# A routed macaron block: second choices by half groups directly behind the first, and both reciprocal roots of the attention stage on VectorE

## What is computed

```python
x = x + 0.5 * ffn(layernorm(x))
x = x + attn(layernorm(x))
x = x + 0.5 * ffn(layernorm(x))

def layernorm(x):  m, v = mean(x), var(x);  return (x - m) / sqrt(v + 1e-5)

def attn(x):       # linear attention, 16 heads of 8 features
    q, k, v = elu(x @ Wq + bq) + 1, elu(x @ Wk + bk) + 1, x @ Wv + bv
    return (q @ (k^T v per head)) @ Wp + bp

def ffn(x):        # 16 experts, the two largest scores of a token, and a shared expert
    scores = softmax(x @ gate_w + gate_b);  top_vals, top_idx = top_k(scores, 2)
    y = sum over the two choices of top_val * ((silu(x @ w1[e] + b1[e]) * (x @ w3[e] + b3[e])) @ w2[e] + b2[e])
    return y + (silu(x @ sw1 + sb1) * (x @ sw3 + sb3)) @ sw2 + sb2
```

## Time and profile before

| what | value |
|---|---|
| time, median of 3 runs | 983.95 us (983.07 to 985.2) |
| profiled execution | 988.44 us |
| its span, first to last instruction | 986.7 us |
| mean granted clock of TensorE | 0.914 |
| busy: TensorE / VectorE / ScalarE / GpSimd | 792.0 / 579.8 / 470.2 / 562.8 us |
| scatters of tokens (L346) | 256, 992 ns each |
| roots on GpSimd (L353, L375) | 16, 28.7 us in all |

### The profile page before, as it was taken

One profiled execution on the slowest core, in us unless ns is written; L12 is line 12 of the kernel. 1 busy time (PEld: TensorE's weight loads), 2 busy tenths in 40 slices (PEclk: granted clock), 3 DMA queues, 4 the chain that ended last, 5 costly groups with the idle time before them and its releaser, 6 DMA issues. The chain is left out here.

```text
span 986.7 us, 20333 instructions
## 1 busy us (share of the span) xinstructions
PE 792.0 (80%) x5348; PEld 705.0 (71%) x5349; DVE 579.8 (59%) x2112; ACT 470.2 (48%) x967; POOL 562.8 (57%) x584
## 2 busy tenths in 40 slices
PE   2899899847999999806788999899934999999920
PEld 2677777737999999804567777787824999999910
DVE  7688876624555555545557776666722555555536
ACT  3356556313555555415456657665302555555500
POOL 1347777762777777722044266575772777776730
PEclk9799999977999999958779999999976999999965
DMA  9912221132333333241021111010132333333349
GB/s 274 141 45 72 65 68 54 52 92 72 100 105 100 105 101 96 83 164 63 1 65 60 49 44 39 31 48 31 50 97 60 96 101 100 103 102 99 96 166 374
DMA packets 83816, 90.45 MB, mean 92 GB/s; under 512 B 20391, under 2 KB 69421, under 8 KB 82733
## 3 DMA queue, kind: packets, MB, share of 16 engines
q1 hardware_dynamic: 64046, 45.41, 18.3%
q0 software_dynamic: 17408, 35.95, 10.8%
q10 hardware_dynamic: 2304, 8.39, 2.1%
HBM read 47.45 MB, written 44.37 MB: 93 GB/s over the span
## 5 line engine op out<-in xcount | busy, mean ns | idle before, releaser
L1246 POOL DMA_INDIRECT ys<-e_y,e_x x288 | 276.5, 960 | 132.0 <-issue 89.0
L346 POOL DMA_INDIRECT xs<-f_xrow,f_slot x256 | 254.0, 992 | 131.9 <-issue 72.8
L1365 PE MATMUL e_py<-w,e_at 97*128 (+1 forms) x1152 | 152.1, 274 | 0.0
L1365 PEld LDWEIGHTS e_py<-w,e_at 97*128 97x128 f32 (+1 forms) x1152 | 139.9, 191 | 0.1
L1270 DVE TENSOR_TENSOR e_a<-e_pu,e_sil 128x352 f32<-128x352 f32 x144 | 75.6, 525 | 98.2 <-ACT e_sil L1296 96.9
L1277 DVE TENSOR_SCALAR e_y<-e_py,e_x 128x128 f32<-128x128 f32 x288 | 87.8, 347 | 58.9 <-PE e_py L1365 57.9
L1290 ACT ACTIVATE e_xth<-e_px 128x256 fp32r<-128x256 f32 x144 | 55.4, 385 | 131.3 <-PE e_px L1329 130.6
L1296 ACT ACTIVATE e_sil<-e_pu 128x352 f32<-128x352 f32 x144 | 66.9, 464 | 91.0 <-PE e_pu L1342 91.0
L1028 PEld LDWEIGHTS f_pz<-sw,f_gated 128*128 128x128 f32 (+1 forms) x768 | 99.4, 191 | 11.4 <-issue 3.2
L1340 PE MATMUL e_pu<-w13h,e_xth 128*128 x288 | 107.2, 372 | 0.0
L843 ACT ACTIVATE f_sil<-f_phg,sb 128x512 f32<-128x512 f32 (+1 forms) x96 | 65.0, 684 | 84.4 <-PE f_phg L1014 83.7
(11 more groups left out here) (166 smaller groups left out, 1362.7 us busy)
## 6 DMA issues: line engine op xcount, KB each, us to landing
e_x<-xs SPq DMA_DIRECT2D x288, 65.0 KB
f_yt<-ys SPq DMA_DIRECT2D x16, 512.0 KB, 4.6
c_yt<-ys SPq DMA_DIRECT2D x8, 1024.0 KB, 10.4
ys<-e_y,e_x POOLq DMA_INDIRECT x288
xa<-in_attn_x ACTq DMA_DIRECT2D x8, 512.0 KB, 10.2
xs<-f_xrow,f_slot POOLq DMA_INDIRECT x256, 2.3
out<-xa ACTq DMA_DIRECT2D x8, 512.0 KB
f_raw<-in_ffn_w SPq DMA_DIRECT2D x32, 88.0 KB
```

What stands on the lines that cost most here:

```text
L346: pool.indirect_dma_start(xs, bass.IndirectOffsetOnAxis(slot[:, q, i:i + 1], 0), xrow[:, i, :], None).then_inc(done, 16)
L1246: pool.indirect_dma_start(ys, bass.IndirectOffsetOnAxis(xin[r][:, t, D:D + 1].bitcast(I32), 0), y[r][:, t, :], None).then_inc(sent[r], 16)
L1365: last = pe.matmul(p_y[r][:, t * D:(t + 1) * D], at[r][0:rows_, q], w2, start=c == 0, stop=c == 1, skip_group_check=True)
```

## The change

First, second choices follow the first choices of their own group, by half groups: GpSimd sends the 8 first choices of group `g`, then the 4 second choices of each half as soon as that half is rewritten. `rewrite` takes a half group `c`; four semaphores count the landed first choices by half groups. In VectorE's order the rewrite of group `s-1` now stands in step `s` of front 0, and in front 1 the first half of group `s` at the end of step `s`, the second half of group `s-1` in step `s` behind `phi_q`. Second, both roots of front 1 are taken on VectorE, each directly behind its variance, with its shift directly behind it; the Newton chain becomes a function `root` for both.

```diff
+        sent0 = [sem(f"f{n}_sent0{r}") for r in range(4)]
 @block.gpsimd
-                def send(g, q, done):
-                    for i in range(g * GT, (g + 1) * GT):
+                def send(c, q, done):
+                    for i in range(c * CHUNK, (c + 1) * CHUNK):
...
-                    send(g, 0, sent0[g % 3])
+                    for c in (2 * g, 2 * g + 1):
+                        send(c, 0, sent0[c % 4])
...
-                    pool.wait_ge(rewrote, g + 1)
-                    pool.sem_inc(passed, 1)
-                    send(g, 1, sent1)
...
-                if n == 0:
-                    for g in range(GROUPS + 1):
-                        first(g)
-                        second_choice(g - 1)
-                else:
-                    for s in range(-3, GROUPS + 2):
-                        first(s - 1)
-                        if 0 <= s + 1 < GROUPS:
-                            scales(s + 1)
-                        if s + 3 < GROUPS:
-                            scales_a(s + 3)
-                        second_choice(s - 2)
+                    for c in (2 * g, 2 * g + 1):
+                        pool.wait_ge(rewrote, c + 1)
+                        pool.sem_inc(passed, 1)
+                        send(c, 1, sent1)
+
+                for g in range(GROUPS):
+                    first(g)
+                    second_choice(g)
 @block.vector
+                def root(y, x, done):
+                    dve.tensor_scalar(half[:], x[:], -0.5, None, ALU.mult)
+                    dve.tensor_scalar(y[:].bitcast(I32), x[:].bitcast(I32), -0.5, MAGIC_ROOT,
+                                      ALU.mult, ALU.add).then_inc(newton, 1)
+                    at = 9 * roots[0]
+                    roots[0] += 1
+                    for i in range(3):
+                        dve.wait_ge(newton, at + 3 * i + 1)
+                        dve.tensor_tensor(sq[:], y[:], y[:], ALU.mult).then_inc(newton, 1)
+                        dve.wait_ge(newton, at + 3 * i + 2)
+                        dve.tensor_tensor(sq[:], sq[:], half[:], ALU.mult).then_inc(newton, 1)
+                        dve.wait_ge(newton, at + 3 * i + 3)
+                        last = dve.scalar_tensor_tensor(y[:], sq[:], 1.5, y[:], ALU.add, ALU.mult)
...
+                def scales_a(g):
+                    wait(dve, xhr_a, 2 * (g - 1))
+                    dve.wait_ge(var_a, g + 1)
+                    root(rs_a[g % 2], ve_a, rstd_a)
...
-                def rewrite(g):
-                    dve.wait_ge(sent0[g % 3], 16 * GT * (g // 3 + 1))
-                    dve.wait_ge(exp2, g + 1)
+                def rewrite(c):
+                    if not 0 <= c < CHUNKS:
+                        return
+                    part = slice(c * CHUNK, (c + 1) * CHUNK)
+                    dve.wait_ge(sent0[c % 4], 16 * CHUNK * (c // 4 + 1))
+                    dve.wait_ge(exp2, c // 2 + 1)
...
 step(s), front 0
                     gates(m)
                     if s == GROUPS:
                         tables()
+                    rewrite(2 * (s - 1))
                     gates(m + 1)
...
                     gates(m + 2)
-                    if s >= 2:
-                        rewrite(s - 2)
+                    rewrite(2 * (s - 1) + 1)
                     if gating:
                         hot(s)
 step_1(s), front 1
-                    if 0 <= s + 2 < GROUPS:
-                        shifts_a(s + 2)
                     if attending:
                         phi_q(a, 0)
                         phi_q(a, 1)
+                    rewrite(2 * (s - 1) + 1)
+                    if attending:
                         phi_k(a, 0)
                         phi_k(a, 1)
                     if gating:
                         largest(s)
...
                         variances(f)
+                        scales(f)
+                        shifts(f)
                     outs(2 * (s - 1) - 1)
                     if gating:
                         sums(s)
                         places(s)
                     gates(m + 2)
-                    if 0 <= s - 2 < GROUPS:
-                        rewrite(s - 2)
                     if b < GROUPS:
                         residual(b)
                     gates(m + 3)
-                    if attending:
-                        shifts(f)
...
                     if b < GROUPS:
                         variances_a(b)
+                        scales_a(b)
+                        shifts_a(b)
                     if gating:
                         low(2 * s)
                     gates(m + 5)
+                    rewrite(2 * s)
                     if gating:
                         low(2 * s + 1)
```

More of the change, by code:

```diff
@@ L116, in build @@
         k.region = sb("region", [P, E])
-        k.nhalf = sb("nhalf", [P, GT])
         k.expert_of = sb("expert_of", [1, SLOT_TILES])
@@ L224, in front @@
             sem(f"f{n}_{m}") for m in names)
-        sent0 = [sem(f"f{n}_sent0{r}") for r in range(3)]
+        sent0 = [sem(f"f{n}_sent0{r}") for r in range(4)]
         def of(g):
@@ L308, in _ @@
                     pool.memset(k.onesb[:], 1.0)
-                    pool.memset(k.nhalf[:], -0.5)
                     pool.memset(k.ones_e[:], 1.0).then_inc(tail, 1)
@@ L348, in send @@
                             None).then_inc(done, 16)
-                def scales(g):
-                    pool.wait_ge(var, g + 1)
-                    wait(pool, xhr, 2 * (g - 2))
-                    pool.tensor_tensor(rs[g % 3][:], ve[g % 2][:], k.nhalf[:], ALU.pow
-                                       ).then_inc(rstd, 1)
                 def first(g):
@@ L421, in variances @@
                                       ).then_inc(var, 1)
-                def scales(g):
-                    y, x = rs[g % 3], ve[g % 2]
-                    wait(dve, xhr, 2 * (g - 2))
-                    dve.wait_ge(var, g + 1)
+                roots = [0]
+                def root(y, x, done):
                     dve.tensor_scalar(half[:], x[:], -0.5, None, ALU.mult)
@@ L439, in scales @@
                             last.then_inc(newton, 1)
-                    last.then_inc(rstd, 1)
+                    last.then_inc(done, 1)
+                def scales(g):
+                    wait(dve, xhr, 2 * (g - 2))
+                    dve.wait_ge(var, g + 1)
+                    root(rs[g % 3], ve[g % 2], rstd)
+                def scales_a(g):
+                    wait(dve, xhr_a, 2 * (g - 1))
+                    dve.wait_ge(var_a, g + 1)
+                    root(rs_a[g % 2], ve_a, rstd_a)
                 def shifts(g):
@@ L512, in places @@
                     dve.tensor_copy(slot[:, :, of(g)], at[:]).then_inc(slots, 1)
-                def rewrite(g):
-                    dve.wait_ge(sent0[g % 3], 16 * GT * (g // 3 + 1))
-                    dve.wait_ge(exp2, g + 1)
-                    if g == 0:
+                def rewrite(c):
[4 more added lines that the diff above has]
+                    dve.wait_ge(exp2, c // 2 + 1)
+                    if c == 0:
                         dve.wait_ge(dests, 1)
-                    dve.scalar_tensor_tensor(xrow[:, of(g), D + 1:D + 2], rec[:, of(g)].unsqueeze(2),
-                                             0.5, wtop[:, of(g)].unsqueeze(2), ALU.mult, ALU.mult)
-                    dve.tensor_copy(xrow[:, of(g), D:D + 1].bitcast(I32),
-                                    dest1[:, of(g)].unsqueeze(2)).then_inc(rewrote, 1)
+                    dve.scalar_tensor_tensor(xrow[:, part, D + 1:D + 2], rec[:, part].unsqueeze(2),
+                                             0.5, wtop[:, part].unsqueeze(2), ALU.mult, ALU.mult)
+                    dve.tensor_copy(xrow[:, part, D:D + 1].bitcast(I32),
+                                    dest1[:, part].unsqueeze(2)).then_inc(rewrote, 1)
                 def low(c):
```

8 lines of the change are left out of this document (removed).

## The result

The changed kernel takes **997.5 us** (median of four runs, 996.7 to 1000.25) against 984.58 before (a median of four; the 983.95 above was that of the first three): a ratio of 1.013, 95% interval 1.0108 to 1.0152. It is slower by some 13 us, outside the predicted range (976 to 993) and on the side that had a chance of 0.31. Its profiled execution took 997.78 us with a span of 996.1, 9.4 us longer than the profiled execution before.

What follows compares the result with a forecast made beforehand. GpSimd's scatter queue was taken to end both fronts, with TensorE, ScalarE and VectorE handing work on inside. Front 0 −8.6, front 1 +2.9 and clock +3.6 gave −2.1 us from 983.95: 981.9 us, range 976 to 993.

Steps and rivals of the forecast that it cites:

- gains nothing here: Front 1, steps 1 to 4: removing TensorE's stall for normalised rows saves nothing, since TensorE then waits for VectorE instead.
- Rival 3: VectorE hides everything: no waits but in steps 6 and 7, both ends gain nearly in full, 965.2 us; chance 0.10.
- the waits of 2 to 5 us in steps 6 to 8 of front 1: Sign expected in the changed profile: VectorE waiting this long at the rewrite for the scatters' DMA.
- 2.3 us to landing by the median: Landing time taken for a half group's last scatter, part of the 12.4 us from slots to second half's rewrite.
- Rival 1: Scatters land late before the second half's rewrite: 13.5 us from slots to rewrite, 993.1 us in all; chance 0.24.
- The term of +1.0: Front 0's price for late rewrites: 0.5 us in step 1 and 0.5 us over steps 2 to 5 together.
- My test for rival 1: Front 0: TensorE's waits for the weight split stay near 1.2 us a step; growth to 2 means rival 1 holds.
- it has 3.11 us to spare: Front 1, steps 1 to 4: VectorE's room for 4.6 us of added work; 1.5 too many, 6.1 us over four steps.
- the +1.8 us for the last stretch: Front 1, step 7 to 8: the rewrite delays the gate product by 4.4 us, of which 2.6 come back.
- step 6 to 7 (+4.9): Front 1: no attention work stands ahead, so VectorE waits in the rewrite before `largest(7)`, 4.9 us later.
- TensorE's clock: Front 1: longer waits lower the granted clock, +2.6 us in step 7 and +1 elsewhere; 3.6, bounds 0 and 7.6.
- The fourth rival: GpSimd and VectorE share an SBUF read port: +2 us for each of eleven roots in front 1, 1004 us; chance 0.03.

Runs made afterwards that it cites:

- scatters_alone: Changed kernel's shorter scatter queue, but front 1's roots stay on GpSimd, its order written out, and rewrites are placed to avoid waits for landings: 962.1 us, ratio 0.9757.
- norm_stats_later: scatters_alone with the norm's root on VectorE behind the first down-product sum, and the next attention group's statistics moved behind the second sum: 956.2 us, ratio 0.9708.
- norm_root: scatters_alone with only the root of the norm ahead of the gate on VectorE, its shift behind it, placed as in the change: 973.4 us, ratio 0.9889.
- all_later: Changed kernel with all rewrites placed later in both fronts, both roots left on VectorE: 979.9 us, ratio 0.9934.
- one_newton: all_later with one Newton step in place of three in each root of front 1: 959.4 us, ratio 0.9736.

## Why the prediction was wrong

**Right.** GpSimd's queue ended both fronts, the half groups took it off the end, and the padding copies are the cap: −9.6 and −13.6 us, confirmed by scatters_alone (−2.4%, 23.8 us). Right was also that VectorE pays, in waits for landings and in room for the roots. That the earlier shift "gains nothing here" held in the changed kernel, but not once the room was there: the way of norm_stats_later is 6.2 us shorter than that of scatters_alone. Rival 3 (VectorE hides everything) was rightly held small. Of the signs named, the waits of 2 to 5 us in steps 6 to 8 of front 1 came as 0.4 to 3.4 us.

**Front 0: the way from slots to rewrite.** The first step that failed is "2.3 us to landing by the median", and with it the 12.4 us. The way was 13.9, since the wait is for the eighth landing and no other, and the eighth met a 1.4 us packet of TensorE's own program in six groups. A median over all scatters cannot show that one place is always late; yet the trace of the kernel before had it: the packet stands there at 67, 89 and 111 us, beside eighth first choices that started at 66.11, 89.02 and 110.53, and where the seven ahead of the last took 2.3 to 2.7 us to land, the view of its line says

```profile
DMA to landing us min/median/max: 3.5/3.5/3.5
```

Rival 1 (landings late, 13.5 us, 993.1) had place and sign, and nearly the price, but the price by luck: its row, set aside because of the copies in flight, has no instruction packet beside it (724 to 729). The term of +1.0 measured 7.4. Of the 7.1 us by which the copies start later, 3.4 are one step in which TensorE waited 2.39 us for the split weights and fell to half clock; the prediction had put the clock into front 1 alone. My test for rival 1, waits for the split near 2 us, was met in three steps (1.82, 2.34 and 2.39).

**Front 1, steps 1 to 4: the room.** The second step that failed is "it has 3.11 us to spare" (busy 14.54 of 17.65 us): it counts the gaps up to the key product. TensorE meets VectorE earlier, at the two sums of the down products: at the first in most steps of the changed kernel (the root starts at 590.10, the sum at 592.26, TensorE waits 2.36 us), at the second when the root stands behind the first. Up to the second the gaps are 1.23 us; what is left behind that sum cannot be used by work that must stand ahead of it. So the norm's root alone was too much, as norm_root shows. Steps 1 to 4 were priced at 6.1 us; from key product to key product they took 5.6, 2.3, 2.6 and 2.0 us longer, 12.5 together, and in all_later, where no rewrite in them waits, still 12.1. Part of this is half clock (below).

**Front 1, the end.** The third step that failed is the +1.8 us for the last stretch, taken from the second half's rewrite alone. It was 8.2: the first half's rewrite of the last group, which the prediction named for front 0 ("lies before gaps") and gave no price here, waited 2.59 us too; behind both TensorE waited 2.47 and 2.91 us, and the 2.6 us that were to "come back" did not, since the products ahead of the tables then ran at half clock. The lateness here is not that of the eighth landing (started at 728.51, 2.3 us): the group's second scatter started 1.4 us late (718.17, then 720.81, where 1.26 us is the usual distance), for a reason that the profile does not show, and the third and fourth took 3.4 and 3.2 us beside the packet. Where most was expected, step 6 to 7 (+4.9), it was 2.9 to the slots; steps 0 to 1 and 5 to 6 came to 1.1 (+1.4) and 3.6 (+2.3). Together the way grew by 28.3 us, where the walk had 16.5 and the clock 3.6.

**TensorE's clock.** This term, +3.6 with bounds 0 and 7.6, was too small: over the whole way the granted clock fell from 0.93 to 0.90, and the same 1397 products kept TensorE busy for 245.3 us in place of 233.9, 11.4 us more. Nor is it a term beside the others. In some steps the waits brought half clock behind them, as in that at 575.24 above (0.95, TensorE busy 1.4 us longer for the same products); in the next, from 608.96, the wait for the sum was nearly as long (2.0 us) and the clock stayed at 1.00. And one_newton gave back more than the roots' own shortening.

**The fourth rival** (a shared port stretches each root by 2 us) did not happen. With GpSimd idle the root at 521.33 took 2.09 us to its shift, beside scatters the one at 532.71 took 2.12. The Trainium skill (Perfetto Trace Analysis, Optimizing Scalar/DVE Operations) says that offloading between GpSimd and VectorE might not help, because they share a read port of SBUF. In these two roots the trace shows no such stretch; what did not help was the order of VectorE's own work.

**The sum.** Forecast −2.1 us. Front 0 came out 5.7 us and front 1 8.0 us worse (first, −2.9 in place of −8.6 by the start of the expert stage's scatters; then +14.5 in place of +6.5 from its first key product to the first loads behind the copies); the rest of the kernel was 2.1 us shorter. That is the 9.4 us between the spans of the two profiled executions; the medians lie 12.9 us apart, because the profiled execution before was 3.9 us above the median of four.

**A version better than both**: norm_stats_later, 956.2 us, a ratio of 0.9708 (0.9677 to 0.9740) to the kernel before. It has the shorter scatter queue of scatters_alone, rewrites behind their landings, the norm's root on VectorE behind the first sum, the attention's root on GpSimd, and the statistics behind the second sum.

## What to carry to other kernels

Give a wait the price of the one transfer that it is for, in its place in the step, and not the median of its kind; then move what waits to where that transfer has landed, which here cost nothing. Count an engine's room only up to the next point at which another engine waits for it, and look for single buffers between the two: gaps behind that point belong to other work. When work is moved to an engine, move something else behind that point with it, or leave it: of two roots of the same length one was free and the other cost 11 us.

## What the runs showed of the hardware

TensorE's program is fetched through the same DMA engines as the data. A 16 KB packet of the instruction queue (27 packets with 0.44 MB in all) lengthened a scatter's landing by 0.6 to 1.8 us (2.9 to 4.1 in place of 2.3). It came at the same place in nearly every step of front 0, because one packet came a step (at 66, 90, 112, 140, 160, 182 and 202 us); 208 waits, already met, ahead of TensorE's work moved it by about 9 us within the step, and the lateness went with it from the eighth scatter to the second.

Of two waits of TensorE at the same place of neighbouring steps, the one of 2.39 us was followed by some 10 us at half clock (granted 0.80 over that step, from 125.05), while the one of 2.34 us left the granted clock at 1.00 (from 101.89):

```profile
101.89:125.05 23.16, 19.85 (x125) 16.41 (x125) 17.63 (x86) 12.91 (x25) 15.44 (x16) 1.00 0.21 63
...
103.16 0.83 PE L1030 MATMUL f_pw<-f_raw,f_centre 128*128 128x352 f32 x2 [2.34 <-DVE w13l L606]
...
126.32 1.26 PE L1030 MATMUL f_pw<-f_raw,f_centre 128*128 128x352 f32 x2 [2.39 <-DVE w13l L606]
```
